# One find product in each TensorE step, and a comparison with two buffers, in a mixture-of-experts tile loop

## The reference

```
idx_flat = topk_idx.reshape(-1)
sort = jnp.argsort(idx_flat)
tok = sort // TOPK
x_sorted = x_flat[tok]
...
g = jax.lax.ragged_dot(x_sorted, we_gate, group_sizes)
u = jax.lax.ragged_dot(x_sorted, we_up, group_sizes)
o = jax.lax.ragged_dot(jax.nn.silu(g) * u, we_down, group_sizes)
y = jnp.zeros_like(x_flat).at[tok].add(o * w_sorted[:, None])
```

## Time and profile before

| | us |
|---|---|
| median of 3 runs | 3974.49 |
| lowest and highest | 3974.14 and 3979.03 |
| the profiled execution's own time | 3973.47 |
| its span, first to last instruction | 3971.7 |
| TensorE products busy | 3650.4 (92%) |
| VectorE busy | 2313.6 (58%) |
| ScalarE busy | 1349.9 (34%) |
| GpSimd busy | 1602.0 (40%) |
| first and last gate product of `expert_tiles` start at | 918.6 and 3929.2 |

### The profile page before, as it was taken

One profiled execution on the slowest core, in us unless ns is written; L12 is line 12 of the kernel. 1 busy time (PEld: TensorE's weight loads), 2 busy tenths in 40 slices (PEclk: granted clock), 3 DMA queues, 4 the chain that ended last, 5 costly groups with the idle time before them and its releaser, 6 DMA issues.

```text
span 3971.7 us, 110141 instructions
## 1 busy us (share of the span) xinstructions
PE 3650.4 (92%) x16856; PEld 2774.8 (70%) x16857; DVE 2313.6 (58%) x5802; ACT 1349.9 (34%) x4031; POOL 1602.0 (40%) x1208
## 2 busy tenths in 40 slices
PE   6809999967999999999999999999999999999996
PEld 3404445536877777787778778787888777787785
DVE  5364555555666665656665565656555666666653
ACT  2212222213333433434333343334333343334331
POOL 1010000004555555555555455555555555455443
PEclk9959999988999999999999999999999999999998
DMA  3322323225666676667666666666666676666654
GB/s 113 106 61 86 98 97 98 96 56 122 125 154 149 153 155 122 149 127 167 141 134 127 158 137 124 138 139 152 124 127 140 122 169 153 140 133 154 137 102 74
DMA packets 216177, 502.40 MB, mean 126 GB/s; under 512 B 46587, under 2 KB 46715, under 8 KB 215360
## 3 DMA queue, kind: packets, MB, share of 16 engines
q0 software_dynamic: 129024, 320.94, 43.4%
q1 hardware_dynamic: 86592, 177.77, 13.6%
q10 hardware_dynamic: 512, 3.15, 0.3%
HBM read 1115.65 MB, written 191.41 MB: 329 GB/s over the span
## 4 chain that ended last, share of the span: by engine, by line
PE 59%; DVE 5%; issue 5%; DVEq 2%; ACT 2%; DMA 2%; ACTq 1%; POOLq 0%; POOL 0%; SPq 0%
PE e_ps_gu L1437 34%; PE e_ps_y L1456 16%; PE e_ps_x L1407 5%; DVE e_w_low L1579 3%; PE e_ps_h L1466 3%; ACT e_w_high L1516 2%; DMA out<-e_y,e_y_ids 2%; PE e_ps_find L1419 1%; DVEq L1301 1%; ACTq L1301 1%; DVE e_past L1611 1%; DVE e_y L1606 1%; DVE e_below L1622 0%; DVEq L1579 0%; ACT e_silu L1535 0%
## 5 line engine op out<-in xcount | busy, mean ns | idle before, releaser
L1381 POOL DMA_INDIRECT out<-e_y,e_y_ids x576 | 935.9, 1625 | 1326.5 <-ACT e_weight L1528 582.4
L1373 POOL DMA_INDIRECT e_x<-token_rows,e_x_ids x576 | 615.9, 1069 | 273.5 <-issue 172.7
L1437 PE MATMUL e_ps_gu<-e_w_high,e_xT_high 128*128 x2304 | 688.4, 419 | 15.1 <-issue 5.1
L1437 PE MATMUL e_ps_gu<-e_w_low,e_xT_high 128*128 x2304 | 646.6, 399 | 6.4 <-issue 4.8
L1437 PE MATMUL e_ps_gu<-e_w_high,e_xT_low 128*128 x2304 | 650.4, 401 | 0.2 <-issue 0.2
L1606 DVE TENSOR_SCALAR e_y<-e_ps_y,e_weight 128x512 f32 (+1 forms) x576 | 430.9, 748 | 243.6 <-PE e_ps_y L1456 202.9
L1587 DVE TENSOR_TENSOR e_xT_low<-e_ps_x,e_xT_high 128x512 fp32r<-128x512 f32 x576 | 397.7, 690 | 286.9 <-ACT e_xT_high L1524 173.6
L1437 PEld LDWEIGHTS e_ps_gu<-e_w_high,e_xT_low 128*128 128x128 f32 x2304 | 428.8, 189 | 128.1 <-issue 29.2
L1437 PEld LDWEIGHTS e_ps_gu<-e_w_low,e_xT_high 128*128 128x128 f32 x2304 | 428.8, 188 | 126.5 <-issue 31.1
L1535 ACT ACTIVATE e_silu<-e_ps_gu 128x256 f32<-128x256 f32 x576 | 221.2, 384 | 821.5 <-PE e_ps_gu L1437 627.0
L1437 PEld LDWEIGHTS e_ps_gu<-e_w_high,e_xT_high 128*128 128x128 f32 x2304 | 396.2, 191 | 98.1 <-issue 37.3
(11 more groups left out here) (245 smaller groups left out, 3926.0 us busy)
## 6 DMA issues: line engine op xcount, KB each, us to landing
e_w_raw<-in_L_ffn_we_gate SPq DMA_DIRECT2D x576, 512.0 KB
e_w_raw<-in_L_ffn_we_up SPq DMA_DIRECT2D x576, 512.0 KB
e_w_raw<-in_L_ffn_we_down SPq DMA_DIRECT2D x576, 512.0 KB
a_x<-in_L_attn_x SPq DMA_DIRECT2D x64, 256.0 KB, 3.4
t_x_in<-in_L_attn_x SPq DMA_DIRECT2D x64, 256.0 KB, 2.8
token_rows<-t_xn SPq DMA_DIRECT2D x64, 256.0 KB, 3.1
out<-t_y_out SPq DMA_DIRECT2D x64, 256.0 KB, 2.0
e_x<-token_rows,e_x_ids POOLq DMA_INDIRECT x576
```

Of the source, the lines that this page charges most:

```text
L1373: pool.indirect_dma_start(x[:, s % XS, :], None, k.rows, bass.IndirectOffsetOnAxis(x_ids[:, s:s + 1], 0)) \
L1381: pool.indirect_dma_start(k.out, bass.IndirectOffsetOnAxis(y_ids[:, s:s + 1], 0), y[:, s % YS, :], None, compute_op=ALU.add).then_inc(adde ...
L1437: last = nc.tensor.matmul(ps_gu[s % 2][:], x[:, s % 2, c, :], w[:, c], start=(n == 0), stop=(n == 3 * DC - 1))
```

## The change

`find` makes one product for one tile, in every step of TensorE, between the turned x and gate/up as before, where it stood with four in every fourth step. The product of the step's tile i + 12 uses the same `ps_find` bank halves; every product now increments `found` by one. The wait for `marked` stands at the first of four, the wait for `picked` at the first and the third. `past` has room for eight tiles, and `mark` writes one half or the other: at s = 2 it marks the four tiles whose first find product stands two steps later. `pick` takes the first pair at s = 1 and the second at s = 3. `expert_of` is called once in each step, after the third product of gate/up, for the next step; in the first of eight steps for that step itself, ahead of its find, and for the next one after the third product.

```
--- before.py
+++ after.py
@@ -1230,7 +1230,7 @@
         hT_high = sb("hT_high", [P, 2, FC, P], F32R)
         hT_low = sb("hT_low", [P, 2, FC, P], F32R)
         y = sb("y", [P, YS, D])
-        past = sb("past", [NB, SHORT, P], BF16)
+        past = sb("past", [NB, UNROLL, P], BF16)
         rest = sb("rest", [P, SHORT])
         below = sb("below", [P, 2, P])
         tokens = sb("tokens", [P, SHORT])
@@ -1410,17 +1410,16 @@
             def expert_of(i):
                 return pe.snap(entry(pe, i, 0, 2 * WSLOTS * E - 1) // (2 * WSLOTS), min_val=0, max_val=E - 1)
 
-            def find(i, experts):
-
-
-                pe.wait_ge(marked, i + SHORT)
-                after(pe, picked, i)
-                for t, e in enumerate(experts):
-                    last = nc.tensor.matmul(ps_find[t // 2][:, t % 2, :], past[:, t, :],
-                                            k.ranks[:, bass.ds(e, 1), :].rearrange("j o t -> j (o t)"), start=True,
-                                            stop=True)
-                    if t % 2 == 1:
-                        last.then_inc(found, 2)
+            def find(i, t, e, slot):
+
+
+                if t == 0:
+                    pe.wait_ge(marked, i + SHORT)
+                if t % 2 == 0:
+                    after(pe, picked, i + t - SHORT + 2)
+                nc.tensor.matmul(ps_find[t // 2][:, t % 2, :], past[:, slot, :],
+                                 k.ranks[:, bass.ds(e, 1), :].rearrange("j o t -> j (o t)"), start=True,
+                                 stop=True).then_inc(found, 1)
 
             def gate_up(i, s):
                 place = words.place(s)
@@ -1475,27 +1474,26 @@
                     words.load(i - 2, s - 2)
                 if s == 0 and third == 2:
                     words.load(i - 1, s - 1)
-                if s % SHORT in (1, 2) and third != 1:
-                    t = 2 * (s % SHORT - 1) + third // 2
-                    if exists(i - s % SHORT + AHEAD_FIND + t):
-                        held[t] = expert_of(i - s % SHORT + AHEAD_FIND + t)
+                if third == 0 and s + 1 < UNROLL and exists(i + 1 + AHEAD_FIND):
+                    held[0] = expert_of(i + 1 + AHEAD_FIND)
 
             def step(i, s):
                 if exists(i + 1):
                     turn_x(i + 1, (s + 1) % UNROLL)
                 if s == 0:
                     words.load(i, s)
-                if s % SHORT == SHORT - 1 and exists(i + 1 - SHORT + AHEAD_FIND):
-                    find(i + 1 - SHORT + AHEAD_FIND, held)
+                    held[0] = expert_of(i + AHEAD_FIND) if exists(i + AHEAD_FIND) else None
+                if exists(i + AHEAD_FIND):
+                    find(i - s % SHORT + AHEAD_FIND, s % SHORT, held[0], (s + AHEAD_FIND) % UNROLL)
                 gate_up(i, s)
                 if exists(i - 1):
                     turn_h(i - 1, (s - 1) % UNROLL)
                 if exists(i - 2):
                     down(i - 2, (s - 2) % UNROLL)
 
-            held = [None] * SHORT
-            for i in range(0, AHEAD_FIND, SHORT):
-                find(i, [expert_of(i + t) for t in range(SHORT)])
+            held = [None]
+            for i in range(AHEAD_FIND):
+                find(i - i % SHORT, i % SHORT, expert_of(i), i % UNROLL)
             turn_x(0, 0)
             walk(pe, step)
             turn_h(TILES - 1, UNROLL - 1)
@@ -1606,9 +1604,9 @@
                 nc.vector.tensor_scalar(y[:, bass.ds(slot, 1), :].rearrange("p o d -> p (o d)"), ps_y[s % 2][:],
                                         weight[:, s % SHORT:s % SHORT + 1], None, ALU.mult).then_inc(y_made, 1)
 
-            def mark(i):
-
-                nc.vector.tensor_tensor(past[:], k.slot_row[:].unsqueeze(1).to_broadcast([NB, SHORT, P]),
+            def mark(i, slot):
+
+                nc.vector.tensor_tensor(past[:, bass.ds(slot, SHORT), :], k.slot_row[:].unsqueeze(1).to_broadcast([NB, SHORT, P]),
                                         k.begin[:, bass.ds(i, SHORT)].unsqueeze(2).to_broadcast([NB, SHORT, P]),
                                         ALU.is_ge).then_inc(marked, SHORT)
 
@@ -1635,12 +1633,12 @@
                     keep_low(i + 1, (s + 1) % SHORT)
                     split_low(i + 1, (s + 1) % SHORT, 0)
                 split_low(i, s, 1)
-                if s == 1 and exists(i - s - SHORT + AHEAD_FIND):
-                    pick(i - s - SHORT + AHEAD_FIND, 2)
-                if s == 2 and exists(i - s + AHEAD_FIND):
-                    mark(i - s + AHEAD_FIND)
+                if s == 1 and exists(i - s + AHEAD_FIND):
+                    pick(i - s + AHEAD_FIND, 0)
                 if s == 3 and exists(i - s + AHEAD_FIND):
-                    pick(i - s + AHEAD_FIND, 0)
+                    pick(i - s + AHEAD_FIND, 2)
+                if s == 2 and exists(i - s + SHORT + AHEAD_FIND):
+                    mark(i - s + SHORT + AHEAD_FIND, slot(SHORT + AHEAD_FIND - s))
                 hidden(i, s)
                 if exists(i - 1):
                     keep_h_low(i - 1, (s - 1) % SHORT)
@@ -1649,10 +1647,10 @@
 
             v.sem_inc(w_low_ready[1], 1)
             for i in range(0, AHEAD_FIND, SHORT):
-                mark(i)
+                mark(i, i % UNROLL)
                 pick(i, 0)
-                if i + SHORT < AHEAD_FIND:
-                    pick(i, 2)
+                pick(i, 2)
+            mark(AHEAD_FIND, AHEAD_FIND % UNROLL)
             words.load(0, 0)
             split_low(0, 0, 0)
             keep_low(0, 0)
```

## The result

The changed kernel takes 4077.71 us (median of 4 runs, 4075.60 to 4079.41), the kernel before on the same chip 3976.28 us: ratio 1.0254, 95% interval 1.0237 to 1.0272. It is 101 us slower. The forecast was 4058 us, within 4015 to 4115.

The account below looks back on a forecast made before the run. TensorE's order was taken to bound the kernel. On the profiled 3973.5 us, 122 - 38 - 21 + 21 = +84 us gave 4057.5; with the median 1.0 us higher, 4058 us, range 4015 to 4115.

Parts of the forecast that it names:

- the saving behind changes of expert: Around changes of expert, the comparison wait (-38 us) and the table reads (-21 us) were to shrink: -59 us together.
- the seam: Each eighth step, at the loop's seam: two more table reads overrun TensorE's spare time by 0.3 us, +21 us, bounds 0 and 57.
- Find products: Between turned x and gate/up: 564 lone products at 0.35 us replace 141 groups at 0.53 us, +122 us.
- The first rival: Lone find products are cheap, occupying TensorE for 0.061 us wherever they stand: 3937 us, chance 0.06.
- The wait for the comparison: TensorE's find waits for VectorE's mark at 34 places; the earlier mark removes this: -38 us, bounds -47 and -15.
- Reads behind a change of expert: Inside gate/up, a third read less and a covered wait save 0.66 us at 32 changes: -21 us, bounds 0 and -35.
- the third rival: TensorE's new time covers nearly all stalls, so the 106 us around changes of expert vanish: 3990 us, chance 0.05.
- At nothing: Items counted as costing nothing: the prologue's extra pick and mark on VectorE, about 1.8 us, and pick and mark in the loop.
- The second rival: Splits and reads hold TensorE as long as mark did, and the seam costs its bound: 4154 us, chance 0.08.

Follow-up runs that it names:

- e3: The changed kernel with past and ranks at 128 partitions, upper 64 zero, so find products have 128 rows: 4008.24 us, 1.0079 of the kernel before.
- e2: e1 with two find products in the third and two in the fourth step of four: 3981.53 us, 1.0012 of the kernel before.
- e1: The kernel before with only the second buffer and earlier mark, find products still four in every fourth step: 3950.05 us, ratio 0.9939.
- e5: The kernel before with two more, unused table reads in the first of eight steps, find products still four in a row: 4020.01 us, 1.0108.
- e7: e1 with find products of 128 rows, the upper 64 zero, four in every fourth step: 3934.55 us, 0.9886 of the kernel before.
- e6: The changed kernel with one buffer of four tiles, mark behind the second pick in VectorE's fourth step: 4174.33 us, 1.0485 of the kernel before.

## Why the prediction was right in sum and wrong in its terms

The sign, the range and the two main mechanisms held. The sum's terms did not: the saving behind changes of expert was put 33 us too small (-59 against -92) and the seam 46 us too cheap, both outside their bounds, and these errors cancelled for the most part. That the sum came to +84 against a measured +101 is in that part luck.

- *Find products, forecast +122, measured +133.* The subtraction gave 0.35 us for a lone product, and it is 0.37: the gap between find and gate/up is 0.16 us for a lone one, its own duration 0.228 against 0.217 us. e3 shows the cause, e2 the price by group. The first rival, cheap lone products, is refuted; with 128 rows a lone product costs 0.12 us, under the 0.13 below which that rival decides, and yet e3 is slower than before, since half of the saving was given back.
- *The wait for the comparison, forecast -38.* e1 shows the waits and the slow issue gone, 40 us between turned x and gate/up, as forecast. But only 25 us reach the end in e1: 7 us came back as stalls inside gate/up, which I left out, 6 between gate/up and turned x, and 2 in the prologue. In the changed kernel 51 us are gone there.
- *Reads behind a change of expert, forecast -21.* This step failed, towards too little: "a third read less saves 0.37 us" in half of the 64 changes. With the term before it, 59 us were forecast and about 92 measured; inside gate/up it was 40 in place of 21. In the place of the earlier trace rows all three stalls are gone, not one of three: as I read it, the find product in each step lets TensorE arrive later at each change, so that its queue has its lead when the reads come. I had written this as the third rival, at its full 106 us, and gave it 0.05; it came to nine tenths. How much of it is the find product's time and how much the more even reads is not fully separated; in e3, with the same reads and less time, gate/up outside the seams loses 33 us in place of 10, so the time is a large part.
- *The seam, forecast +21, bounds 0 and 57; measured +67*, outside the bounds. The step that failed is "one of the four reads took 0.845 us; if it was only held up by a full queue, 0.54 us of slack is hidden in it". There is none. In the trace of the changed kernel 28 of the seam steps have no slow read (all six together within 0.1 us of 6 x 0.31), and from their first to their last gate product it is 3.17 us in the median, 0.49 more than elsewhere: just the plain count of 1.25 - 0.75 = 0.5 us. In the 17 where reads take 0.5 to 0.8 us longer in all, as the one of 0.873 us above does, it is 3.70. So a slow read goes into the step in full, and the mean is 0.95 us. e5 gives 0.84 us for the two reads alone.
- *At nothing.* The prologue took 1.5 us, not 0. Pick and mark cost TensorE next to nothing, as said: turned h waits for `e_hT_low` 4.1 us in all, in place of 2.9.

The second rival, waits replaced in full at the splits, did not come: gate/up waits for the split (e_w_low) 1.3 us in all, in place of 4.1. Its other half, the seam at its bound of 57 us, did.

## What to carry to other kernels

A small product between large ones can cost far more than its columns, here 0.25 of 0.37 us for the change between 64-row and 128-row weights: look in the timeline at the distances on both sides of it, keep such products together, or pad their rows with zeros up to the neighbours' form. A wait that disappears from an engine whose queue reads registers may be worth less or more than its length: count the lead that the queue has behind it, and put reads where the lead is long. And two parts of one change should be tried apart, each without the other: the second buffer is worth 25 us to products in groups of four (e1) and 97 us to lone ones (e6), and the lone products cost about 126 us with it and 196 us without.

## What the runs showed that was not expected

- A lone bf16 product of 64 rows by 130 columns between float32 products cost 0.37 us of TensorE's time, with 128 rows 0.12 us (e3); four in a row 0.53 and 0.29 us (e7).
- Two table reads that nobody used, in one step of eight, made the kernel 1.1% slower (e5), though a read's load takes 0.3 us and 0.75 us seemed to be spare.
- A wait that ended 1.3 us before its product was due still cost 0.5 us further on: the queue had stood at it, and started its next read 0.7 us later relative to the gate products (e6).
